# A convolution's SiLU by ScalarE's own function, two chunks in a row, in a Mamba and soft-mixture kernel on one core

## The reference

```python
xf, res = jnp.split(x @ in_proj_w.T, [D_INNER], axis=-1)      # D_INNER = 512
xf = jax.nn.silu(_causal_dw_conv(xf, conv_w, conv_b))
y = _ssm(xf, res, x_proj_w, dt_proj_w, dt_proj_b, A_log, D)
xb = jax.nn.silu(_causal_dw_conv(xf, conv_b_w, conv_b_b))
y_b = _ssm(xb, res, ..., reverse=True)
y = y + y_b                                                    # then @ out_proj_w.T

def _selective_scan(u, dt, A, B, C, D, reverse=False):         # dt = softplus(...)
    dA, dB_u = einsum('bld,dn->bldn', dt, A), einsum('bld,bld,bln->bldn', dt, u, B)
    dA_shift = jnp.pad(dA[:, 1:], ...)
    dA_cum = jnp.exp(flip(cumsum(flip(dA_shift, 1), 1), 1))
    xs = jnp.cumsum(dB_u * dA_cum, 1) / (dA_cum + 1e-12)
    return einsum('bldn,bln->bld', xs, C) + u * D
```

## Time and profile before

| | |
|---|---|
| median of 3 runs | 5855.48 us (5845.51 to 5856.24) |
| the profiled execution | 5838.37 us, span 5836.5 us |
| mean granted TensorE clock | 0.929 |
| busy: PE, DVE, ACT, POOL | 86%, 79%, 70%, 75% of the span |
| first scan to last scan (L1000) | 91.1 to 4821.3 us, 1024 scans |

### The profile page before, as it was taken

The page is one execution under the profiler, slowest core; times in us unless marked ns, Lnnn a source line. Parts: engine busy times, 40 slices in busy tenths (PEclk is TensorE's granted clock), DMA queues, the critical chain, the costliest instruction groups (busy, mean ns, idle before and its releaser), DMA issues. The chain is left out here.

```text
span 5836.5 us, 50669 instructions
## 1 busy us (share of the span) xinstructions
PE 5031.1 (86%) x14640; PEld 2563.0 (44%) x14640; DVE 4622.5 (79%) x4109; ACT 4081.5 (70%) x6431; POOL 4362.3 (75%) x2136
## 2 busy tenths in 40 slices
PE   6888888888888888888888878787889787999999
PEld 3444443434343434344444434343434344656578
DVE  6898989898989898989898989898989992222235
ACT  4888888888888888888888888887878883111100
POOL 4898989898989999999999999999998981000000
PEclk8999989898989999999898989898989898999999
DMA  2444434444444444444444444344444442343356
GB/s 88 128 133 127 136 124 134 128 133 128 133 129 129 132 133 131 129 128 133 126 131 128 135 127 134 127 132 131 124 138 124 137 126 78 99 138 122 98 171 216
DMA packets 555604, 755.29 MB, mean 129 GB/s; under 512 B 124091, under 2 KB 272443, under 8 KB 553277
## 3 DMA queue, kind: packets, MB, share of 16 engines
q1 hardware_dynamic: 540765, 737.36, 41.1%
q10 hardware_dynamic: 14560, 14.68, 0.8%
HBM read 662.04 MB, written 89.82 MB: 129 GB/s over the span
## 5 line engine op out<-in xcount | busy, mean ns | idle before, releaser
L643 POOL TENSOR_TENSOR g_ring<-dtu,b_ring 128x1024 f32<-128x1024 f32 x1026 | 2418.9, 2369 | 271.6 <-DVE e_ps L1000 246.1
L1000 DVE TENSOR_TENSOR_SCAN e_ps<-e_ps,g_ring 128x1024 f32<-128x1024 f32 x1024 | 2343.3, 2288 | 11.8 <-POOL g_ring L643 11.8
L1156 PE MATMUL y_ps<-v_ring,ident 128*128 128x512 f32 x3088 | 1626.3, 636 | 235.1 <-DVE res_gate L983 189.9
L652 POOL TENSOR_TENSOR v_ring<-z_ring,c_ring 128x1024 f32<-128x1024 f32 x768 | 1816.7, 2368 | 0.0
L796 ACT ACTIVATE e_ps<-dt,a_neg 128x512 f32<-128x512 f32 x2050 | 1327.9, 680 | 458.1 <-DVE v_own L1022 298.3
L806 ACT ACTIVATE f_ring<-rsum,consts,a_neg_half 128x512 f32<-128x512 f32 x2052 | 1550.9, 805 | 36.7 <-DVE e_ps L1013 33.7
L1156 PEld LDWEIGHTS y_ps<-v_ring,ident 128*128 128x128 f32 x3088 | 589.3, 204 | 889.6 <-issue 807.4
L1013 DVE SCALAR_TENSOR_TENSOR z_ring<-f_ring,e_ps 128x1024 f32<-128x1024 f32 x768 | 935.6, 1218 | 50.8 <-issue 1.7
L1156 PE MATMUL y_ps<-v_own,ident 128*128 128x512 f32 x1028 | 533.8, 614 | 0.0
L1089 PE MATMUL side<-u,conv_diag 128*128 128x512 f32 x1088 | 494.6, 597 | 20.7 <-ACT disp_ring L757 11.3
L1326 ACT ACTIVATE x_act<-x_ps,x_bg 128x512 f32<-128x512 f32 x128 | 87.9, 687 | 570.2 <-PE x_ps L1385 570.2
(11 more groups left out here) (133 smaller groups left out, 5180.1 us busy)
## 6 DMA issues: line engine op xcount, KB each, us to landing
b_ring<-bc_scr SPq DMA_DIRECT2D x1027, 256.0 KB, 3.7
c_ring<-bc_scr SPq DMA_DIRECT2D x1025, 256.0 KB, 3.4
pT_scr<-rowT_ring SPq DMA_DIRECT2D x136, 256.0 KB, 4.1
m_pT<-pT_scr SPq DMA_DIRECT2D x16, 2048.0 KB, 8.5
sT_scr<-sT_ring SPq DMA_DIRECT2D x272, 64.0 KB, 2.8
x_xT<-sT_scr SPq DMA_DIRECT2D x16, 1024.0 KB, 9.3
eo_scr<-x_eo SPq DMA_DIRECT2D x32, 512.0 KB, 5.1
m_eo<-eo_scr ACTq DMA_DIRECT2D x14, 1024.0 KB, 7.1
```

Of the source, the lines that this page charges most:

```text
L643: pool.tensor_tensor(g_ring[:, k], dtu[d][:], both(b_ring[:, k:k + 1]), ALU.mult).then_inc(g_done, 1)
L652: pool.tensor_tensor(v_slot(i), z_ring[:, k], both(c_ring[:, k:k + 1]), ALU.mult).then_inc(v_pool, 1)
L1000: dve.tensor_tensor_scan(e, e, g, 0.0, ALU.mult, ALU.add).then_inc(scan_done, 1)
L1156: pe.matmul(y_ps[:, t % 2], ident[:], v, start=(t % (TILES // PAIRS) < 2), stop=True, skip_group_check=True).then_inc(v_used, 1)
```

## The change

- `b_conv` holds the bias itself, not its half. The SiLU of a chunk is one activation (`ACT.Silu`) from the bank into `u`, by ScalarE alone; it releases the bank. It is done for two chunks together, when the second one's turn has come (lag 3 of the odd chunk). VectorE's product (L924) is gone.
- In the prologue the two dt0 slots come before the first chunk of conv1, since its chunks now stand in a row.
- `ON_DVE` is {0, 4, 8, ..., 60} in place of {1, 5, 9, ..., 61}, and `EARLY` (20, 52) in place of (21, 53).
- `DTU_LAG` goes from 3 to 4 and `CUT_LAG` from 5 to 6.
- `normalize` follows the side work of tile 29.
- The slot of v is looked up with the number of the step over all sequences; with 16 steps on VectorE and 48 on GpSimd in each, 4 and 6 slots, it is the same slot as before.

```diff
-    ("x0", 0), ("conv1", 0), ("dt0", 0), ("dt0", 1)) + tuple(("conv1", i) for i in range(1, 4)) + (("x1", 0),)
+    ("x0", 0), ("dt0", 0), ("dt0", 1)) + tuple(("conv1", i) for i in range(4)) + (("x1", 0),)
...
-    DTU_LAG, RSUM_LAG, CUT_LAG = 3, 3, 5
-    EARLY = (21, 53)
-    ON_DVE = [i for i in range(STEPS) if i % 4 == 1]
+    DTU_LAG, RSUM_LAG, CUT_LAG = 4, 3, 6
+    EARLY = (20, 52)
+    OWN = 16
+    ON_DVE = [i for i in range(STEPS) if (i * OWN + OWN // 2) // STEPS != ((i - 1) * OWN + OWN // 2) // STEPS]
...
-                    elif kind in ("conv0", "conv1"):
-                        bias = b_conv_half[:, d, i:i + 1]
-                        act.activation(u[d][:, i, PAD:], src, ACT.Identity, scale=0.5, bias=bias).then_inc(half_done, 1)
-                        act.wait_ge(half_done, at.nth(s, ("conv0", "conv1")))
-                        act.activation(src, src, ACT.Tanh, scale=0.5, bias=bias).then_inc(tanh_done, 1)
+                    elif kind in ("conv0", "conv1") and i % 2 == 1:
+                        act.activation(u[d][:, i - 1, PAD:], side[:, at.bank(s - 1)], ACT.Silu,
+                                       bias=b_conv[:, d, i - 1:i]).then_inc(side_free[at.bank(s - 1)], 1)
+                        act.activation(u[d][:, i, PAD:], src, ACT.Silu, bias=b_conv[:, d, i:i + 1]).then_inc(free, 1)
...
+                    for s in range(SLOTS):
+                        side_step(at, s, t - tile_of[s])
                     if t == APPLY_TILE:
                         normalize(b)
-                    for s in range(SLOTS):
-                        side_step(at, s, t - tile_of[s])
...
-            dve.tensor_scalar(b_conv_half[:], b_conv_half[:], 0.5, None, ALU.mult)
...
-                if kind in ("conv0", "conv1") and lag == 4:
-                    d = int(kind[-1])
-                    dve.wait_ge(tanh_done, at.nth(s, ("conv0", "conv1", "res")))
-                    dve.scalar_tensor_tensor(out=u[d][:, i, PAD:], in0=src, scalar=1.0,
-                                             in1=u[d][:, i, PAD:], op0=ALU.add, op1=ALU.mult).then_inc(free, 1)
```

More of the change, by code:

```diff
@@ L290, in sequence_stage @@
         w_in = sb("w_in", [P, KM, 2 * DI])
-        b_conv_half = sb("b_conv_half", [P, NDIR, KI])
+        b_conv = sb("b_conv", [P, NDIR, KI])
         w_x = sb("w_x", [P, NDIR, KI, XR])
@@ L357, in sequence_stage @@
         tanh_done = sem("tanh_done")
-        half_done = sem("half_done")
         dt_done, dtu_done, cut_done = sem("dt_done"), sem("dtu_done"), sem("cut_done")
@@ L443, in _ @@
                 sp.dma_start(dst, src).then_inc(w_loaded, 16)
-            for dst, src in ((b_conv_half, conv_b), (w_x, x_wT), (a_neg, A_log)):
+            for dst, src in ((b_conv, conv_b), (w_x, x_wT), (a_neg, A_log)):
                 sp.dma_start(dst[:], src).then_inc(w_loaded, 16)
@@ L650, in times_c @@
                 pool.wait_ge(z_done, b * STEPS + (i + 1 + CR))
-                pool.wait_ge(v_used, b * TILES + (2 * (same_slot_before(i) + 1) + CR))
-                pool.tensor_tensor(v_slot(i), z_ring[:, k], both(c_ring[:, k:k + 1]), ALU.mult).then_inc(v_pool, 1)
+                pool.wait_ge(v_used, 2 * (same_slot_before(b * STEPS + i) + 1) + CR)
+                pool.tensor_tensor(v_slot(b * STEPS + i), z_ring[:, k], both(c_ring[:, k:k + 1]), ALU.mult).then_inc(v_pool, 1)
             def variances(now):
@@ L916, in side_step @@
                 if kind == "res" and lag == 3:
-                    dve.wait_ge(tanh_done, at.nth(s, ("conv0", "conv1", "res")))
+                    dve.wait_ge(tanh_done, at.nth(s, ("res",)))
                     dve.scalar_tensor_tensor(out=res_gate[:, i], in0=res_gate[:, i], scalar=1.0, in1=src,
                                              op0=ALU.add, op1=ALU.mult).then_inc(free, 1)
-                if kind in ("conv0", "conv1") and lag == 4:
-                    d = int(kind[-1])
-                    dve.wait_ge(tanh_done, at.nth(s, ("conv0", "conv1", "res")))
-                    dve.scalar_tensor_tensor(out=u[d][:, i, PAD:], in0=src, scalar=1.0,
-                                             in1=u[d][:, i, PAD:], op0=ALU.add, op1=ALU.mult).then_inc(free, 1)
                 if kind in ("dt0", "dt1"):
@@ L1020, in times_c @@
                     dve.wait_ge(c_loaded[k], b * (RING.count(k) * 16) + (RING[:i].count(k) + 1) * 16)
-                    dve.wait_ge(v_used, b * TILES + (2 * (same_slot_before(i) + 1) + CR))
-                    dve.tensor_tensor(v_slot(i), e_ps[:, i % 2], both(c_ring[:, k:k + 1]), ALU.mult).then_inc(v_dve, 1)
+                    dve.wait_ge(v_used, 2 * (same_slot_before(b * STEPS + i) + 1) + CR)
+                    dve.tensor_tensor(v_slot(b * STEPS + i), e_ps[:, i % 2], both(c_ring[:, k:k + 1]), ALU.mult).then_inc(v_dve, 1)
                 for t in range(TILES):
@@ L1154, in add_state @@
                         pe.wait_ge(y_gated, b * PAIRS + (t // (TILES // PAIRS) + 1))
-                v = v_slot(i)[:, t % 2]
+                v = v_slot(b * STEPS + i)[:, t % 2]
                 pe.matmul(y_ps[:, t % 2], ident[:], v, start=(t % (TILES // PAIRS) < 2),
```

## The result

The changed kernel takes 5797.6 us (median of 4 runs, 5797.1 to 5799.6); the kernel before took 5852.6 beside it (4 runs, 5845.5 to 5856.2). The ratio is 0.9908, with a 95% interval of 0.9891 to 0.9925: 0.9% faster. The forecast was 5802 us. The profiled execution took 5797.46 us, its span is 5795.7, and the first and last scan start at 92.4 and 4783.5 us, 39.1 us less apart than before in its profiled execution.

What follows compares the result with a forecast made beforehand. GpSimd's work plus its idle time was taken to bound the loop. Terms 1.9 + 0.7 - 1.0 + 1.1 + 0.6 = 3.3 us a sequence, x 16 = 53 us off 5855.5, gave 5802 us; range 5750 to 5865 (forecast case 5770 to 5835).

Steps and rivals of the forecast that it cites:

- The frame: Whole loop: GpSimd's work plus its idle brackets set the time; savings from step 52 to next sequence's step 18 worth nothing.
- Normalization 1.9: Head of the step 19 chain: rstd one v earlier, so xn starts earlier; 1.9 us a sequence gained.
- guard 0.7: At cols0: guard of step 23 needs step 20, not 21, ending TensorE's idle time; 0.7 us a sequence gained.
- own product 1.1 + 0.6: VectorE's product leaves the front of scan 30 (1.1 us at step 31); likewise at step 39 (0.6 us).
- dtu 0: Steps 4, 19, 50 become 5, 20, 51: softplus wait at step 50 only changes its name; 0 us gained.
- The waits named for v 49 and v 51: Step 50 region: GpSimd would wait 2.3 us at v 49 and 2.4 at v 51, in place of 4.86.
- Silu -1.0: conv0_0/1 and conv1_0/1: TensorE idles for the bank held over two chunks; 1.0 us a sequence lost.
- rival C: Slower, 5889 us: ScalarE's loads back to Exp delay scans at conv1_0/1 and conv1_2/3; chance 0.11.
- A's full gain: Rival A: dtu's waits at steps 50 and 19 really go, 7 us a sequence, 5740 us; chance 0.13.
- B's stall of TensorE: Rival B: TensorE's bank hold costs 3.6 us, eating the chain's gain; 0.7 a sequence left, 5844 us; chance 0.12.
- D: Rival: each ScalarE table switch drains and costs 2.7 us, 11 us more a sequence on ScalarE; 5890 us; chance 0.02.
- Busy times: Whole run: VectorE loses 93 us of products; ScalarE gains 73 us net from table loads and Silu.

Runs made afterwards that it cites:

- the experiment on the hold: Changed kernel with one Tanh per chunk in its own turn in place of the Silu pair, no bank held past its turn: 5739.8 us, ratio 0.9803.

## Why the prediction was right, and which of its terms were not

**The number came true, 4 us off, by two errors that cancel, and that is luck.** The three parts without Silu brought 6.2 us a sequence where 4.3 was counted, and Silu cost 2.8 to 3.3 where 1.0 was.

**The frame held in part.** That the loop is GpSimd's work and its brackets is true as a sum, and the brackets fell by the 2.8 us a sequence that the loop gained. The conclusion drawn from it, that nothing saved or lost from step 52 to step 18 is worth anything, is wrong. "No other engine has that much in the loop" left VectorE out of account: it idles 27.0 us of the 296.3 of a sequence, GpSimd 24.8. From step 54 to 15 it is VectorE that sets the pace, and from 15 to 19 it is the normalization's chain: dtu alone gained 1.8 us there and the normalization 0.6, in a stretch in which GpSimd has next to no bracket.

**Normalization 1.9, guard 0.7, own product 1.1 + 0.6: 4.3 predicted, 6.2 measured.** The own steps, dtu and the normalization together brought 5844.8 - 5745.7 = 99 us, 6.2 a sequence. The own steps do nearly all of it. By the table of the scans they gained 2.2 from scan 15 to 19 (the rstd, 1.9 counted), 1.1 from 19 to 24 (the guard, 0.7), 1.0 from 24 to 30 (the own product of step 29, 1.1) and 2.0 from 30 to 38, where 0.6 was counted for that of step 37. Of these 2.0, 1.0 to 1.2 are the product at the same clock. The prediction took off half of it for the v that GpSimd gets, but behind the wait GpSimd has time for that v. The rest goes with TensorE's clock, 3.4 us at its lower level in place of 9.0, which the prediction has no term for. It also has none for the clock from scan 15 to 24, where the lower level went from 18.9 to 16.3 us. Going by the kernel's own sequences, 2.5 us more of the lower level come with 1.2 us more time, so about 1.3 of the 3.4 us gained there are the clock's (an estimate). The rstd comes a v earlier by the own steps alone: in that kernel xn waits for L117 once, 2.5 us in all. Moving `normalize` then adds nothing.

The brackets of the earlier trace rows are also those of a sequence with a short wait: 21.3 us were added up from it, where the mean is 24.0. The forecast doesn't rest on that sum.

**dtu 0: right in the change (nothing in the loop), wrong alone (42 us).** The waits named for v 49 and v 51, 2.3 and 2.4 us, are there with 1.82 and 2.38. The one at v 19 (2.14) was folded into the chain and not expected as a row of its own, so L652 shows 6.3 us a sequence in place of 4 to 5. What the argument missed is that an earlier GpSimd brings the rstd of step 13 earlier. In the change xn no longer waits for it, so that is worth nothing there; in the kernel before it did, and dtu alone brought xn 1.7 us forward against scan 13.

**Silu -1.0: wrong in size and in kind; -2.8 to -3.3 measured, inside its bounds.** The prediction charged TensorE's wait for the held bank, at rowsT0 and slots0. TensorE's waits for the Silu in the kernel after (us, times, longest):

```profile
PE side L1088 <- ACT u L718: 3.0, 2, 1.5
PE side L1083 <- ACT u L716: 2.2, 1, 2.2
```

That is 5.2 us in three waits of the whole run, and none comes back in each sequence; the experiment on the hold says the same. What costs is the loads, 53 us of 164, most of it (2.6 of 3.4 us a sequence) at the two pairs conv1_0/1 and conv1_2/3. That is rival C's mechanism, and the pairs that it named. Scan 50 waits for `e_ps` at 2086.70, and there are 64 such waits in the run, at steps 16, 25, 47 and 50 of each sequence; the one at step 16 is there without Silu too.

```profile
DVE e_ps L994 <- ACT e_ps L796: 33.9, 64, 0.8
```

C's size was too large. It counted both loads of these pairs, 2 x 2.57, and 1.3 behind them, 6.4; 1.4 and 1.2 were measured, about one load each. At these two pairs ScalarE still waits 1.5 and 1.1 us for the convolution behind the load ahead of Silu, so that load is hidden and the one back is left. No run takes away only one of the two. The prediction had found ScalarE 2 us ahead of each scan, and by that counted nothing for the loads between scans 24 and 30; that step was wrong. A's full gain and B's stall of TensorE did not come.

**D fell.** The softplus's load begins at 2090.46 and the softplus at 2091.75: 1.29 us for a switch, with no gap ahead of it. The Trainium skill ("ScalarE: Activation LUTs", What ACT_TABLE_LOAD costs) adds a drain of about 1.38 us to each; the trace does not show it here either.

**Busy times.** ScalarE +82 us against +73 predicted: Silu takes 0.685 in place of 0.67 (2 us), and the rest is overlap that a busy time of the engine counts once. VectorE -63 against -93 for the same reason: L924's 93 us are gone, but its ends overlapped its neighbours'.
